# Edge attention with the split values as stationary operand, edge counts as logarithms, and the mixing product moved to another stage

## What is computed

```python
qkv = x @ W_qkv.T + b_qkv
Q, K, V = jnp.split(qkv, [DK * HEADS, 2 * DK * HEADS], axis=-1)      # 8 heads of 64
scores = jnp.einsum('ehd,ehd->eh', Q[receivers], K[senders]) * scale
smax = jax.ops.segment_max(scores, receivers, num_segments=n_nodes)
ex = jnp.exp(scores - smax[receivers])
denom = jax.ops.segment_sum(ex, receivers, num_segments=n_nodes)
att = ex / denom[receivers]
out = jax.ops.segment_sum(att[:, :, None] * V[senders], receivers, num_segments=n_nodes)
msg.reshape(n_nodes, HEADS * DV) @ W_ff.T + b_ff
# added to x with the layer's token mixing, whose weights the kernel folds into one 512 x 512 matrix "mix":
x = x + _L1_gnn_ref(xn, ...) + _L1_mix_ref(xn[None], ...)[0]
```

## Time and profile before

| | us |
|---|---|
| median of 3 runs | 2469.54 |
| lowest, highest | 2468.75, 2473.69 |
| the profiled execution | 2472.86, of which its span 2471.3 |
| TensorE busy in the span | 2188.1 (89%) |
| VectorE, ScalarE, GpSimd busy | 1348.4, 761.9, 774.4 |
| stage_prepare | about 0 to 262 |
| layer 0 | about 262 to 1260 |
| norm and token mixing | about 1260 to 1405 |
| projections | 1405 to 1510 |
| edge attention | 1510 to 1920 |
| join | 1921 to 2004 |
| experts | 2004 to 2471 |

### The profile page before, as it was taken

The page is one execution under the profiler, slowest core; times in us unless marked ns, Lnnn a source line. Parts: engine busy times, 40 slices in busy tenths (PEclk is TensorE's granted clock), DMA queues, the critical chain, the costliest instruction groups (busy, mean ns, idle before and its releaser), DMA issues. The chain is left out here.

```text
span 2471.3 us, 31984 instructions
## 1 busy us (share of the span) xinstructions
PE 2188.1 (89%) x9448; PEld 1316.1 (53%) x9449; DVE 1348.4 (55%) x3843; ACT 761.9 (31%) x1750; POOL 774.4 (31%) x862
## 2 busy tenths in 40 slices
PE   8977889889889889999879896999999984999992
PEld 4334444444444444444334454999998542777771
DVE  4874077877878778879754022666666321100012
ACT  2034122332333322323321111666666110222220
POOL 0000056667667666667710000111110003111113
PEclk9998999999999999999989898999999985999996
DMA  4013189999999999999960153442421032222424
GB/s 142 11 64 138 55 305 374 334 375 367 347 364 364 353 366 357 365 357 387 399 233 0 35 157 97 120 128 81 126 82 57 31 120 77 104 104 106 170 104 135
DMA packets 153614, 487.48 MB, mean 197 GB/s; under 512 B 21908, under 2 KB 22580, under 8 KB 153392
## 3 DMA queue, kind: packets, MB, share of 16 engines
q0 software_dynamic: 100720, 358.29, 39.1%
q1 hardware_dynamic: 52800, 128.08, 15.8%
HBM read 449.64 MB, written 36.66 MB: 197 GB/s over the span
## 5 line engine op out<-in xcount | busy, mean ns | idle before, releaser
L547 POOL DMA_INDIRECT m_ring<-in_table,m_rows_at x640 | 642.5, 1004 | 324.4 <-PE m_acc L792 159.6
L792 PE MATMUL m_acc<-m_ring,m_diag 128*128 128x512 f32 x1280 | 606.0, 626 | 88.4 <-ACT m_diag L714 87.4
L792 PEld LDWEIGHTS m_acc<-m_ring,m_diag 128*128 128x128 f32 x1280 | 248.6, 199 | 416.3 <-issue 271.5
L607 DVE CUSTOM_DVE_ANT_0 m_ring<-m_ring,m_coming,m_part 128x512 f32<-128x512 f32 x640 | 441.4, 748 | 33.1 <-DMA m_ring<-in_table,m_rows_at 22.5
L714 ACT ACTIVATE m_diag<-ident,m_inner 128x128 f32<-128x128 f32 x640 | 218.5, 394 | 104.8 <-DVE m_inner L607 104.2
L1231 PE MATMUL a_psT<-v,a_pT 128*128 128x128 f32 x1600 | 199.8, 280 | 4.7 <-ACT a_pT L1321 0.5
L1231 PEld LDWEIGHTS a_psT<-v,a_pT 128*128 128x128 f32 x1600 | 184.9, 192 | 23.0 <-ACT a_pT L1321 22.9
L1775 PEld LDWEIGHTS e_psU<-e_rowsT,x_w 128*128 128x128 f32 x1472 | 170.7, 195 | 13.4 <-issue 13.4
L1775 PE MATMUL e_psU<-e_rowsT,x_w 128*128 128x128 f32 x1472 | 171.1, 278 | 2.1 <-DVE e_rowsT L1806 1.1
L691 ACT ACTIVATE m_qz<-m_psQ,m_bq 128x128 f32<-128x128 f32 x80 | 29.3, 366 | 455.1 <-PE m_psQ L768 455.1
L1784 PE MATMUL e_psY<-x_w,e_hT 128*128 128x512 f32 x368 | 161.7, 592 | 0.0
(11 more groups left out here) (305 smaller groups left out, 2632.6 us busy)
## 6 DMA issues: line engine op xcount, KB each, us to landing
x_w<-in_we SPq DMA_DIRECT2D x16, 2048.0 KB, 11.3
a_mask<-edge_masks SPq DMA_DIRECT2D x40, 320.0 KB, 2.9
a_cnt<-edge_counts SPq DMA_DIRECT2D x40, 320.0 KB, 2.9
m_ring<-in_table,m_rows_at POOLq DMA_INDIRECT x640, 6.2
qk_parts<-p_parts SPq DMA_DIRECT2D x32, 320.0 KB, 4.3
a_k<-qk_parts SPq DMA_DIRECT2D x32, 320.0 KB, 7.6
edge_shares<-shareT SPq DMA_DIRECT2D x10, 640.0 KB, 3.0
m_share<-edge_shares SPq DMA_DIRECT2D x10, 640.0 KB, 7.1
```

The costliest lines, as they stand in the source:

```text
L547: pool.indirect_dma_start(ring[:, slot, :], None, ins["table"], bass.IndirectOffsetOnAxis(rows_at[:, h, k:k + 1], 0)).then_inc(s_land[slot ...
L607: dve.tensor_tensor_reduce(ring[:, slot, 0:D], ring[:, slot, 0:D], coming[:, t % 2, :], part[:, b, k:k + 1], 0.0, ALU.mult, ALU.add, inner ...
L792: pe.matmul(acc[:, :], diag[:, h % 2 * TOPK + k, :], ring[:, nth % RING, D:2 * D], start=h + k == 0, stop=h * TOPK + k == HEADS * TOPK - 1 ...
```

## The change

- In stage_prepare the mask goes: no L353, no store of it. TensorE waits for the copied counts where it waited for the mask.
- In the projections q is scaled by +1/8. ScalarE takes the logarithm of each tile's counts, VectorE puts -1e30 where the count is 0, SP loads the counts and stores the result as f32, `edge_log_counts`; SP does one tile after each chunk, the last two at the end, all ahead of the values on VectorE. The values are split into f32r and remainder, by head. After them stands the product with `mix`, added to x. The join's weight loads go to the attention stage.
- In the attention VectorE adds the logarithms of the counts to the score (which psS has one buffer for), writes the sum to `prob` and takes its maximum (as the minimum of the negative); Exp reads `prob`, and ScalarE sums as it goes: `weigh` is gone. A transposed piece goes twice to SBUF, rounded by ScalarE (`high`) and its remainder by VectorE (`rest`). The value product has the split values stationary (64 columns of a head and 64 of remainders) and the two parts of `pT` moving, for two tiles with the same head at once, 256 columns. Its 128 rows are copied (`keep_sums`), and a matmul with two identities on top of each other (`fold`) adds the halves and turns them back. The loops are written out.
- In the join the product with `mix` is gone.

```diff
@@ stage_prepare, ScalarE
                 act.activation(cnt16[:, b, :], C2[b][:, 0:NP], ACT.Copy, accum_out=deg[:, b:b + 1]).then_inc(s["cnt_out"], 1)
-                act.activation(mask[:, b, :], C2[b][:, 0:NP], ACT.Relu, bias=unlinked[:, :], scale=NEG).then_inc(s["masked"], 1)
@@ stage_projections, SyncE
+            for t in range(2):
+                load_counts(t)
             for i in range(2 * PAIRS):
                 sp.wait_ge(s["split"], i + 1)
...
+                save_log(i)
+                load_counts(i + 2)
+            for t in range(2 * PAIRS, NT):
+                save_log(t)
@@ stage_projections, TensorE
+            for t in range(NT):
+                pe.wait_ge(s["vout"], min(NT, NT - 1 + t))
+                if t >= 2:
+                    pe.wait_ge(s["yout"], t - 1)
+                for k in range(KC):
+                    mm = pe.matmul(psV[:, t % 2, :], c.xnT[:, k, t * P:(t + 1) * P], mix[:, k, :], start=k == 0, stop=k == KC - 1)
+                mm.then_inc(s["y"], 1)
@@ stage_projections, VectorE
+            def unlinked(t):
+                dve.wait_ge(s["log"], t + 1)
+                dve.tensor_scalar(none[:, :], cnt[:, t % 2, :], 0.0, NEG, ALU.is_equal, ALU.mult)
+                dve.drain()
+                dve.tensor_tensor(log_cnt[:, t % 2, :], log_cnt[:, t % 2, :], none[:, :], ALU.add).then_inc(s["masked"], 1)
+                dve.drain()
...
                 dve.tensor_tensor(parts[:, b, 1, :], full[:, b, :], parts[:, b, 0, :], ALU.subtract).then_inc(s["split"], 1)
+                unlinked(i)
+            for t in range(2 * PAIRS, NT):
+                unlinked(t)
             for t in range(NT):
                 dve.wait_ge(s["v"], t + 1)
-                dve.tensor_tensor(v[:, t, :], psV[:, t % 2, :], bv[:, :], ALU.add).then_inc(s["vout"], 1)
...
+                dve.tensor_tensor(v_row[:, t % 2, :], psV[:, t % 2, :], bv[:, :], ALU.add).then_inc(s["vout"], 1)
+                dve.drain()
+                rows = v_row[:, t % 2, :].rearrange("p (h d) -> p h d", h=HEADS)
+                dve.tensor_copy(v[:, t, :, 0, :], rows)
+                dve.drain()
+                dve.tensor_tensor(v[:, t, :, 1, :], rows, v[:, t, :, 0, :], ALU.subtract)
@@ stage_edge_attention, TensorE
+            def turn(n, piece):
+                a, z = THIRDS[piece]
                 if piece == 0:
+                    pe.wait_ge(s["exp"], n + 1)
+                if n:
+                    pe.wait_ge(s["rest"], 3 * n - 2 + piece)
...
+            def sums(g, piece):
...
+                pe.wait_ge(s["rest"], 6 * g + 4 + piece)
...
+            for n in range(UNITS):
+                g = n // 2
+                if n % 2 == 0 and g:
+                    sums(g - 1, 1)
+                turn(n, 0)
+                if n % 2 == 0 and g:
+                    sums(g - 1, 2)
+                turn(n, 1)
+                turn(n, 2)
+                if n + 2 < UNITS:
+                    score(n + 2)
+                if n % 2:
+                    sums(g, 0)
+                elif g:
+                    add_halves(g - 1)
@@ stage_edge_attention, VectorE
+            for n in range(UNITS):
+                rest(n, 0)
+                rest(n, 1)
+                if n + 2 < UNITS:
+                    lowest(n + 2)
+                rest(n, 2)
+                if n % 2:
+                    shares(n // 2)
@@ stage_edge_attention, ScalarE
+            for n in range(UNITS):
+                g = n // 2
+                high(n, 0)
+                high(n, 1)
+                if n % 2 == 0 and g:
+                    keep_sums(g - 1)
+                if n + 1 < UNITS:
+                    exponent(n + 1)
+                if n % 2 and g:
+                    message(g - 1)
+                high(n, 2)
@@ stage_join, TensorE
-                    for k in range(KC):
-                        pe.matmul(psO[:, t % 2, :], c.xnT[:, k, t * P:(t + 1) * P], mix[:, k, :], start=k == 0, stop=False)
                     pe.wait_ge(s["mT"], t + 1)
```

More of the change, by code:

```diff
@@ L1160, in load_keys @@
                 if m >= 2:
[L1161 removed]
+                    sp.wait_ge(s["score"], (m - 1) * 2 * NT)
                 for h in range(2):
@@ L1253, in _ @@
-            pe.wait_ge(s["k0"], 128)
-            for i in range(3):
-                score(0, i, 0)
-            for piece in range(2):
-                turn(0, 0, piece)
-            for m in range(PAIRS):
-                with pe.Fori(0, J - 1) as j:
-                    group(m, j, m)
-                group(m, J - 1, m + 1 if m + 1 < PAIRS else None)
+            def sums(g, piece):
+                m, t, h = unit(2 * g)
+                a, z = THIRDS[piece]
+                pe.wait_ge(s["rest"], 6 * g + 4 + piece)
+                if piece == 0 and g:
+                    pe.wait_ge(s["both"], g)
+                for x in range(a, z):
+                    for part in range(2):
+                        mm = pe.matmul(psU[:, 0:2 * P], v[:, x, 2 * m + h, :, :].rearrange("p a d -> p (a d)"),
+                                       pT[:, part, x, :, :].rearrange("p t n -> p (t n)"),
+                                       start=x + part == 0, stop=x + part == NT)
+                if piece == 2:
+                    mm.then_inc(s["sums"], 1)
@@ new lines, in add_halves @@
+            def add_halves(g):
+                pe.wait_ge(s["both"], g + 1)
+                if g:
+                    pe.wait_ge(s["msg"], 2 * g)
+                for b in range(2):
+                    mm = pe.matmul(psM[:, 64 * b:64 * b + 64], both[:, b, :], fold[:, :], start=True, stop=True)
+                mm.then_inc(s["folded"], 1)
+            score(0)
+            score(1)
+            pe.wait_ge(s["fold"], 1)
+            for n in range(UNITS):
[13 more added lines that the diff above has]
+                    add_halves(g - 1)
@@ L1263, in _ @@
+            sums(UNITS // 2 - 1, 1)
+            sums(UNITS // 2 - 1, 2)
+            add_halves(UNITS // 2 - 1)
         @block.vector
         def _(dve):
[L1265 to L1279 removed]
@@ L1343, in _, with exponent @@
-            exponent(0, 0)
-            exponent(1, 1)
-            for piece in range(2):
-                keep_turned(0, 0, piece)
-            with act.Fori(0, GROUPS - 1) as g:
-                for i in range(GROUP):
-                    step(g, i, False)
-            for i in range(GROUP):
-                step(GROUPS - 1, i, True)
-def stage_join(c, msg, mix, weights, ahead):
+            def exponent(n):
+                act.wait_ge(s["low"], n + 1)
+                act.activation(prob[:, n % 2, 0:N], prob[:, n % 2, 0:N], ACT.Exp, bias=low[:, n % 2:n % 2 + 1], scale=-1.0,
+                               accum_out=den[:, n % 4:n % 4 + 1]).then_inc(s["exp"], 1)
@@ L1357, in stage_join @@
+            keep_sums(UNITS // 2 - 1)
+            message(UNITS // 2 - 1)
+def stage_join(c, msg, weights, ahead):
     nc = c.nc
```

311 lines of the change are left out of this document (139 added, 172 removed).

## The result

The changed kernel takes 2433.93 us (median of 4 runs, 2430.15 to 2439.88), the kernel before, run beside it, 2471.61 (2468.75 to 2473.92). The ratio is 0.985, its 95% interval 0.9835 to 0.9867. The forecast was 2454: the direction was right, and the time lies in the range, but the gain is 37.7 us where 16 were forecast. The profiled execution of the changed kernel took 2439.88 with a span of 2438.2, 6 us above its median.

A forecast was written before the change was run, and what follows sets the result against it. A closed loop through the engines, no single engine, was to bound the changed attention. Terms -24.8 + 2 - 11 + 34.3 + 11 - 34.3 + 6.7 = -16.1 us gave 2456.8 from the profiled 2472.9, so 2454; range 2432 to 2476.

The forecast's parts named there:

- Attention: Edge attention stage: 4.49 us per unit against 4.80, -24.8 us over 80 units, and +2 at its start.
- the closed loop: Attention: score, minimum, last subtraction, transposes, next score; 4.04 and 4.94 us, together 8.98 per pair, set the pace.
- the start: Beginning of the attention: low clock, hidden less by one score buffer than by two; +2 us (0 to 5).
- The engines' own work: Attention, per unit: TensorE 3.54 us, VectorE 3.6, ScalarE about 3.2; none was expected to set the pace.
- Dearer handoffs: Rival, attention: waits between engines cost more than measured rows say; 4.72 us per unit, 2472 us in all; chance 0.19.
- Cheaper ones: Rival, attention: handoffs between engines cost less than the rows say; 4.2 us per unit, 2430 us in all; chance 0.07.
- Clock: Rival, attention: TensorE's clock falls to 1.2 GHz; about 2660 us if wholly, 2495 if every second pair; chance 0.08.
- two passes: Rival, attention: the f32r value product takes two passes; 5.4 us per unit, 2525 us in all; chance 0.04.
- Prepare: Prepare stage: without ScalarE's mask pass, TensorE's and VectorE's waits shrink; -11 us (-8 to -15).
- Projections: Projection stage: the mixing product moved in adds 34.3 us, and a TensorE gap before the values +11 (+5 to +16).
- The gap: Projections: TensorE waits 9 us for the last tiles' counts, logarithm and mask; 2 more for the fallen clock.
- Join: Join stage: mixing product gone, -34.3 us; lost cover for ScalarE's message copies, +6.7 (+4 to +9).

The follow-up runs named there:

- after: The changed kernel itself, with all of the described change, profiled and run beside the kernel before: 2433.93 us, ratio 0.985.
- the three sets: Groups in which the follow-up kernels were run, each beside the kernel before, which took 2584, 2572 and 2469 us.

## Why the prediction was right or wrong

- **Attention, -22.8 forecast, -44.0 measured.** The mechanism was right: the closed loop from the score over the minimum and the last subtraction to the next score, shown by what it cost to lengthen it (34 us), by what the same work cost beside it (0), and by what went when it was cut and its followers removed (47 us). One thing about it was not as I read it: I had TensorE idle 0.95 us in each unit, and it is idle 0.6 on average, nearly all of it in the short unit. In the long one the path (4.94 in my sum, 4.69 measured) lies just above TensorE's own 4.64. The step that failed is the sizes of its links. From score to minimum I took 1.63, and the trace of after has 1.47 and 1.58; the minimum I took as 1.72, to its end and that of the small instruction behind it, but the subtraction starts 0.08 after that instruction has begun, so 1.62. Over a pair that is 0.2 for the first and 0.2 for the second: 8.53 and not 8.98, or 4.27 per unit, outside my bounds of 4.30 to 4.70 and the 4.4 to 4.6 that I had named as the sign of being right. I had named the second as a bound ("the minimum's hand-over could be 0.1 shorter"), and then not taken it into the value. Why the first link is shorter stays open; its matmuls and the minimum itself last as long as before (1.41, and 1461 for 1460 ns), and from the modelled end of the last matmul to the minimum it is 0.19 in the kernel before, 0.15 for one head of a pair and 0.04 for the other now. The links together make 80 x 0.22 = 18 us of the 21; the rest is the start, for which I had added 2, and the ends of the stage.
- **The engines' own work.** TensorE's is 3.65 us per unit for the 3.54 of the sum: the f32r matmuls of the value product stand 0.12 apart and not 0.112, and the folding takes 0.4 per pair and not 0.3. VectorE's terms as written make 3.76 and not 3.6; it is busy 3.4 in the trace. The forecast hung on neither.
- **The rivals.** Dearer handoffs: the opposite is true. Cheaper ones, at 4.2 per unit, were nearest (4.27) and got 0.07. I put the fixed order of the instructions against them, and the eight waits more per pair in favour of dearer ones; no link became longer by these waits. Clock and two passes: out, by 0.99 and by 287 ns. The Trainium skill, page TensorE: Matmul & The Clock Gate, "Part 4: PE-mode transpose", states that a transpose does not count as busy in the way a matmul does. The earlier trace rows speak against it, as the clock rose behind transposes alone; and in the attention, with some 30% of TensorE's work in transposes, the clock stayed at 0.99, so such a rule cost nothing here.
- **Prepare, -11 forecast, -14.7 measured** in the stage, within -8 to -15: 13.2 less to the last one-hot load and 1.5 less behind it, the one pass at the end that I had put at 1.2. Of the 13.6 of VectorE's waits that I had set as an upper end 12.3 went (18.2 to 5.9); I had counted on 8.4. The other 1.9 of the first row of the table lie in work that the change doesn't touch, 1.6 of them in front of the first one-hot load.
- **Projections, +45.3 forecast, +49.4 measured.** The 34.3 of the product are there. The gap is 12.0 for 9, and some 2.6 at half the clock behind it, as forecast. The step that failed in size is the load of tile 9's counts: I let it land in 2.9, the row of a load in the attention, and it took 5.9 (issued at 1466.53, used at 1472.45). That is no matter of this one load: the ten of the stage took 4.7 to 5.9, the middle one 5.6.
- **Join, -27.6 forecast, -25.9 measured.** The cover was worth 8.4 and not 6.7. The waits for the copies are 6.5 of it: six of 0.83 where I had seven of 0.9, 0.25 for 0.4 in the first tile, and 1.26 in the last. What the other 1.9 are isn't shown; the granted clock was 0.97 in the stage, for 0.99 before.
- **The sum** came out too small by 17 in the profiled execution, and by 22 in the medians (37.7 for 16). The range, 2432 to 2476, held by 2 us, and by luck: the attention's -44.0 lies outside its own bounds (-40 to -8, and 0 to 5 for the start), and the projections, the join and the unchanged last stage, which came out 4.1, 1.7 and 4.0 dearer, took back a part of it.

## What to carry to other kernels

Where no engine is full, write down the closed loop through all engines, and measure its links from the start of one instruction to the start of the next: here an end lay up to 0.1 us behind the next start, and the ends taken for starts made 8 of the 21 us missed. Do it for each unit of the pattern by itself: 90% busy was one unit in which TensorE was full and one with 1.2 us of idle time. A cut loop gives back nothing until the next one is looked for: moving the last subtraction and ScalarE's copies cost 9 us, and with the two things that then stood in the way it saved 47. And work that leaves a stage takes its cover along: look what waited behind it, and mend that order at once (6 us here).

## What the runs showed of the hardware that was not expected

- ScalarE's and VectorE's writing of f32r costs next to nothing over f32: the copy of 512 columns is 597 ns for 598 in the earlier trace rows, of 256 columns 390 for 384, the subtraction 689 for the 692 of the addition in the earlier trace rows.
- Exp out of SBUF and with a running sum takes 1341 ns, 43 more than out of PSUM and without one (1298); which of the two makes the 43 isn't shown. The read of the sum behind it takes 199 ns and begins 0.11 us before Exp's end.
- The loads of 320 KB of counts landed in 5.6 us (median of ten) in the projections, for 2.9 in the attention of the kernel before.
- Layer 0 with its gathered rows took about 100 us more in two of the three sets (1008 to 1038 us from its first to its last matmul on them, for 915 to 919 in the other profiles), in every profile whatever the kernel, while the attention of the changed kernel kept its length to 0.1 us. The kernel before wasn't profiled in those sets; its whole times, 2584 and 2572 for 2469, fit.
